# Key requests three tiles ahead in place of four, and group bounds made one step earlier, in a graph layer with attention and feed-forward

## What is computed

```python
xn = layernorm(x)
h = xn @ W
norm = dinv[src] * dinv[dst]                 # dinv from the degrees
gnn = relu(segment_sum(h[src] * norm, dst) + b)
Q, K, V = heads(xn Wq'), heads(xn Wk'), heads(xn Wv')     # 16 heads of 64
phiQ, phiK = elu(Q) + 1, elu(K) + 1
S = phiK^T V ; Z = sum(phiK)
mix = (phiQ S / (phiQ Z + eps)) Wo' + bo
x = x + gnn + mix
x = x + ffn(layernorm(x))                    # gated, three hidden products
```

## Time and profile before

| | us |
|---|---|
| median of 3 runs | 998.29 |
| lowest, highest | 996.62, 1002.45 |
| the profiled execution | 997.37 |
| its span, first to last instruction | 995.5 |
| TensorE busy with matmuls | 972.9 (98%) |
| VectorE, ScalarE, GpSimd busy | 533.6, 291.3, 142.5 |

### The profile page before, as it was taken

How to read it: one execution, slowest core, us unless ns; L and a number is a source line. 1 busy time by engine, 2 the same in 40 slices (tenths; PEclk the granted TensorE clock), 3 DMA queues, 4 the chain that set the end, 5 groups by cost and what they waited for, 6 DMA issues and landing times.

```text
span 995.5 us, 13214 instructions
## 1 busy us (share of the span) xinstructions
PE 972.9 (98%) x4841; PEld 821.7 (83%) x4841; DVE 533.6 (54%) x1004; ACT 291.3 (29%) x553; POOL 142.5 (14%) x190
## 2 busy tenths in 40 slices
PE   5999989999999999999999999999999999999998
PEld 4887867887889989978786788767788999999986
DVE  6786567768644788782112555547557212122354
ACT  6772114223223343241212212114113312135300
POOL 7101001001011050050300000000201103064100
PEclk9999998999999999999999999999999999999999
DMA  7412013113011012122201465536422302010053
GB/s 267 149 52 85 4 30 103 43 31 102 29 40 60 27 72 91 52 69 95 74 34 49 147 185 185 164 125 185 169 80 88 125 1 85 1 43 1 22 189 138
DMA packets 50871, 86.81 MB, mean 87 GB/s; under 512 B 22924, under 2 KB 27276, under 8 KB 50784
## 3 DMA queue, kind: packets, MB, share of 16 engines
q1 hardware_dynamic: 42304, 57.27, 17.6%
q0 software_dynamic: 8480, 28.45, 8.8%
HBM read 61.60 MB, written 24.09 MB: 86 GB/s over the span
## 4 chain that ended last, share of the span: by engine, by line
PE 92%; DVE 4%; DMA 1%; ACT 1%; issue 1%; POOL 1%; DVEq 0%; ACTq 0%; POOLq 0%
PE PS L1450 11%; PE PS L1452 11%; PE PS L1451 11%; PE PS L1574 9%; PE PS L1573 9%; PE PS L1575 9%; PE PS L1631 5%; PE PS L1633 4%; PE PS L1652 3%; PE PS L1651 3%; PE PS L1650 3%; PE PS L1465 2%; PE PS L1703 2%; PE PS L1704 2%; PE PS L1702 2%; PE PS L1492 2%
## 5 line engine op out<-in xcount | busy, mean ns | idle before, releaser
L1450 PE MATMUL PS<-ring,act_t 128*128 128x512 f32 (+1 forms) x480 | 195.8, 408 | 1.5 <-POOL ring L457 0.6
L1452 PE MATMUL PS<-ring,act_t 128*128 128x512 f32 (+1 forms) x480 | 191.3, 399 | 0.0
L1451 PE MATMUL PS<-ring,act_t 128*128 128x512 f32 (+1 forms) x480 | 191.0, 398 | 0.0
L1573 PE MATMUL PS<-act_t,ring 128*128 128x416 f32 (+1 forms) x432 | 159.5, 369 | 1.4 <-POOL ring L457 1.3
L1574 PE MATMUL PS<-act_t,ring 128*128 128x416 f32 (+1 forms) x432 | 152.4, 353 | 0.0
L1575 PE MATMUL PS<-act_t,ring 128*128 128x416 f32 (+1 forms) x432 | 151.9, 352 | 0.0
L1450 PEld LDWEIGHTS PS<-ring,act_t 128*128 128x128 f32 (+1 forms) x480 | 90.4, 188 | 24.5 <-POOL ring L457 2.0
L1452 PEld LDWEIGHTS PS<-ring,act_t 128*128 128x128 f32 (+1 forms) x480 | 89.9, 187 | 22.6
L1451 PEld LDWEIGHTS PS<-ring,act_t 128*128 128x128 f32 (+1 forms) x480 | 90.3, 188 | 21.3 <-issue 0.5
L1573 PEld LDWEIGHTS PS<-act_t,ring 128*128 128x128 f32 x432 | 81.4, 188 | 6.8 <-issue 3.4
L1574 PEld LDWEIGHTS PS<-act_t,ring 128*128 128x128 f32 x432 | 81.5, 189 | 4.0 <-issue 3.4
(11 more groups left out here) (195 smaller groups left out, 1656.8 us busy)
## 6 DMA issues: line engine op xcount, KB each, us to landing
stage_x<-in_wslices_dram POOLq DMA_DIRECT2D x54, 256.0 KB, 4.0
stage<-in_wslices_dram POOLq DMA_DIRECT2D x42, 256.0 KB, 3.5
xr<-x_d SPq DMA_DIRECT2D x18, 512.0 KB, 3.7
phin_d<-phiq SPq DMA_DIRECT2D x8, 625.0 KB, 3.2
xrow<-in_x_dram SPq DMA_DIRECT2D x9, 512.0 KB, 3.6
xh<-in_x_dram SPq DMA_DIRECT2D x18, 256.0 KB
x_d<-xh SPq DMA_DIRECT2D x18, 256.0 KB
x_d<-xr SPq DMA_DIRECT2D x9, 512.0 KB, 2.9
```

The source lines that it names most:

```text
L1450: pe.matmul(out_ap, node_rows(0, k, t), ring[:, slot(k0 + k), 0, :], start=(k == 0), stop=False)
L1451: pe.matmul(out_ap, node_rows(1, k, t), ring[:, slot(k0 + k), 0, :], start=False, stop=False)
L1452: ins = pe.matmul(out_ap, node_rows(0, k, t), ring[:, slot(k0 + k), 1, :], start=False, stop=(k == KD - 1))
L1573: pe.matmul(out_ap, w[0], x_t[:, 0, k, o:o + n], start=(k == 0), stop=False)
```

## The change

Two edits. SyncE requests the keys of three tiles before the first count store, and after the store of tile `dt` those of tile `dt + 3`; `kraw` keeps its four places. And VectorE makes the bounds in step 9 and the constants in step 10, in place of the other way round.

```diff
 KEY_BUFS = 4
+KEYS_AHEAD = 3
...
-            for dt in range(KEY_BUFS):
+            for dt in range(KEYS_AHEAD):
                 keys_load(dt)
...
                     sp.dma_start(ct_d[dt], ctile[:, dt % 2].rearrange("p a b -> p (a b)")).then_inc(ct_stored[dt % 2], 16)
-                    if dt + KEY_BUFS < NT:
-                        keys_load(dt + KEY_BUFS)
+                    if dt + KEYS_AHEAD < NT:
+                        keys_load(dt + KEYS_AHEAD)
...
-            edge_parts = {4: edge_rows, 6: edge_order, 7: edge_keys, 8: edge_starts, 9: edge_constants, 10: edge_bounds}
+            edge_parts = {4: edge_rows, 6: edge_order, 7: edge_keys, 8: edge_starts, 9: edge_bounds, 10: edge_constants}
```

## The result

| | before | after |
|---|---|---|
| median, 6 runs each | 998.07 | 990.83 |
| lowest, highest | 995.50, 1002.45 | 989.51, 991.29 |
| the profiled execution | 997.37 | 989.64 |
| its span | 995.5 | 987.7 |

The ratio is 0.9923, with an interval from 0.9901 to 0.9946: 7.7 us faster, between 5.4 and 9.9 (the medians lie 7.2 apart). In a later measurement, the last of the experiments, the same two kernels gave 0.994 (0.9924 to 0.9957), 6.0 us.

What follows compares the result with a forecast made beforehand. TensorE was taken to bound the kernel, standing still for a copy behind tile 0's late store. 6.36 + 0.22 - 0.1 = 6.5 us gave 990.9 from the profiled time, 991.8 from the median; forecast 991.4, range 989.5 to 995.0.

Steps and rivals of the forecast that it cites:

- What bounds the kernel: Step 18: TensorE waits 3.8 us for ScalarE's first tile 2 copy, held by tile 0's store, 15.4 us in SyncE's queue.
- The fit to 0.02 us: Tile 0's store landed at 149.33 and ScalarE's copy started at 149.35, so the store was taken as its release.
- Three tiles ahead: 39 key requests before tile 0's store in place of 52, 36.2 us, leaving SyncE free at 132.8.
- bounds in step 9: Swapping bounds and constants on VectorE moves everything on SyncE up to the store 5.21 us earlier, at no cost.
- Either part alone would do too: Store lands at 137 with three tiles ahead, 144.1 with the bounds; TensorE needs the copy at 145.8; gains don't add.
- What the wait is worth: Step 18 into the following product: 6.36 us, of which 4.0 standing still and 2.35 at half clock.
- the low clock appears only behind this wait: Reason for counting 2.35 us at half clock, granted clock 0.50 from 150 to 152, as part of the gain.
- The first wait for keys: VectorE's 2.49 us wait for tile 0's keys goes; worth 0.22 us on TensorE in step 13, ends 0 and 0.22.
- Later keys: Tile 3's keys, requested behind tile 0's store, land by 149 and are needed at 155: slack 6 us, cost 0.
- What the standing still had covered: VectorE in steps 18 to 20 moves only about 5.0 us earlier; cost between 0 and 0.4 us, taken as 0.1.
- The branch: Before tile 2's count on VectorE: a possible instruction fetch could lengthen the 0.21 us gap towards 2.13; sum 6.2, not 6.5.
- Everything behind moves as a whole: All work after step 21 (queries, aggregation, feed-forward) starts on TensorE's progress, so it keeps the whole gain.

Runs made afterwards that it cites:

- the third place: The kernel before with three places for finished counts in place of two, SyncE's queue order and the bounds unchanged; 991.18 against 996.82, ratio 0.9943.
- the runs with 2.86 and 8.01 us of standing still: Bounds in step 9 alone, plus six or twelve unread transfers on SyncE before tile 0's store; steps 12 to 21 took 66.64 and 73.04 us against 62.38.
- the two kernels with late bounds: The kernel before with three tiles ahead alone (990.38), and with three places for finished counts (991.18), against 996.82; bounds still in step 10.
- the repetition of after: The changed kernel with both edits measured again beside the kernel before on one chip; 989.43 against 995.81, ratio 0.994.
- one of 1.4 us: Bounds in step 9 alone, plus three unread transfers on SyncE before tile 0's store; steps 12 to 21 took 63.91 us against 62.38.

## Why the prediction was right, point by point

*What bounds the kernel.* Right. The store of tile 0 in SyncE's queue held ScalarE, and ScalarE held TensorE. The fit to 0.02 us was the argument, the third place the proof.

*Three tiles ahead; bounds in step 9.* Right, with the requests a little quicker than taken (35.36 for 39, not 36.2). Both edits alone did what was worked out for them. For the bounds alone the copy was to be done 1.4 us ahead of TensorE's need; it was 0.13, since TensorE's need lay 1.9 us earlier in this run (143.88 for 145.82) while the store's issue, 139.10, lay only 1.1 earlier than the 140.2 worked out (the 52 requests took 48.92 us and not 48.29), and since the store took 4.2 us to land. The working also left out the time from the copy to TensorE's start, which takes the 0.13 away. "Either part alone would do too" came true for this part by luck; stated with the scatter of its terms it should have been a near thing.

*What the wait is worth.* 6.36 expected, 6.36 measured (6.60 less 0.24). The two halves of it, 4.0 standing and 2.35 at half clock, were both rightly counted; in the same count the runs with 2.86 and 8.01 us of standing still put 1.4 and 2.65 on top. The sentence under it, that the low clock appears only behind this wait, was wrong. Between 22 and 24 us the clock granted of before was at 0.50 as well, and I had not seen it because the page's digit is a 9 from 90% on. It didn't touch the sum, but it is why the two profiled executions are 7.73 us apart and not 6.2.

*The first wait for keys.* 0.22 expected, 0.24 measured, and the two kernels with late bounds are 0.3 slower for it.

*Later keys.* Cost 0 expected and 0 measured. Tile 3's last request was issued by 142.1 and, as the requests around it land in at most 2.1 us, landed by 144.2, 9 us before its use at 153.15. That is more than the 6 us worked out, since I had counted 14.7 us from the store to the last request, which took 13.6, and 3.9 for landing.

*What the standing still had covered.* Term 0.1, measured 0. The key instruction of step 19 moved from 159.98 to 153.15; less the 1.54 of the start and the 0.24 of the keys that is 5.05, where 5.0 was taken. VectorE is indeed later against TensorE (its lead in step 19 is 6.83, TensorE's at the count matmuls of that step 8.1), and TensorE doesn't wait for it; its one wait of 0.2 us for a one-hot tile is at 237 us in after and 245 in before, in step 31 both times. The branch that the Trainium skill (Runtime: NRT & Kernel Launch, Instruction fetch mechanics) warns of did not make the gap longer here: at tile 2 it went from 0.21 us to none, and at tile 6 it is 2.16 after 2.13. So in these two kernels tile 6 has the long gap and tile 2 the short one, whether VectorE had stood still before or not. What makes the gap no row shows, a fetch or something else.

*Everything behind moves as a whole.* Nearly. VectorE's marks are 8.14 earlier up to the queries and 8.11 in the product of the graph layer (543 us), and 7.75 at the first sum of the aggregation. The 0.4 in between went in the small products with the output weights, which take their weights from transfers just landed. From their start to the next product it is 8.02 us before (542.01 to 550.03) and 8.40 after (533.90 to 542.30). The second eight of them, each with the wait in front:

```profile
545.92 3.92 PE L1614 MATMUL PS<-wo_sb,st_blk 128*128 128x512 f32 x8 [0.20 <-DMA wo_sb<-in_wo_dram]
```

```profile
537.87 4.19 PE L1615 MATMUL PS<-wo_sb,st_blk 128*128 128x512 f32 x8 [0.26 <-DMA wo_sb<-in_wo_dram]
```

The edit isn't needed for that. The same stretch took 8.26 us in the repetition of after, 8.11 and 8.06 with one edit alone, and 8.32 with the third place, which has neither edit. It varies from one profiled execution to the next; why, is open.

*The number.* 991.4 was forecast, 990.83 measured. The gain of the steps, 6.6, and the ratios (7.7 us for the changed kernel at first and 6.0 in the later measurement, 6.2 and 5.8 for the single edits) are one result within their intervals. The nearest figure for the edit itself is the trace's, 6.6 in the steps and 6.2 at the end of the span (7.73 less 1.54).

## What to carry to other kernels

An engine's queue that issues transfers in order is a resource: work requested early for later use, here four tiles of keys at 0.93 us a request, delays a small transfer behind it that frees a buffer now. Ask of each queued transfer who waits for it and by when, and request ahead only as far as the requests need to land in time; three tiles sufficed, two were 49 us slower than three and 43 slower than before. Idle time for which the trace names no engine could be read here by listing the code's waits at that instruction and adding each one's landing time to its issue.

## What was unexpected of the hardware

A pause of TensorE of 2.7 us brought a granted clock of 0.52 in the stretch from 148 to 150 and cost 1.6 us beyond itself; one of 1.4 us left the clock at 1.00 and cost 0.2. The pause of 7.8 us cost 2.8 beyond itself, hardly more than that of 3.8 with 2.5. Each of these is one execution, and the same pause need not have the same effect: after 1.78 us of standing still, near 22 us and some 13 us after TensorE had begun, before was granted 0.50 and after 1.00. That is 1.5 us of 995 that belong to no edit, and that a comparison of two single profiled executions takes for a result.
